# A recurrence of 512 coupled oscillators behind a GRU: VectorE's queue put in another order, the fourth stage's q kept in PSUM, and a clip that waits for ScalarE's square

## The reference

```python
# GRU cell, once per time step, h is [4, 512]
gi = x @ W_ih + b_ih
gh = h @ W_hh + b_hh
r = sigmoid(i_r + h_r);  z = sigmoid(i_z + h_z)
n = tanh(i_n + r * h_n)
h_new = (1.0 - z) * n + z * h

# coupled system, four times per time step, q and p are [4, 512]
i_couple = tanh(q) @ coupling.T
dq = q - q ** 3 / 3.0 - p + drive + i_couple + bias
dp = EPSILON * (q + ALPHA - BETA * p)
# after the four stages
q_next = clip(q + DT / 6 * (dq1 + 2 * dq2 + 2 * dq3 + dq4), -20, 20)
p_next = clip(p + DT / 6 * (dp1 + 2 * dp2 + 2 * dp3 + dp4), -20, 20)
```

## Time and profile before

| | us |
|---|---|
| median of 3 runs | 3659.93 (3659.13 to 3660.63) |
| the profiled execution, its own time | 3661.45 |
| its span, first to last instruction | 3659.7 |
| busy in it: PE | 3546.2 (97%) |
| busy in it: DVE | 2998.4 (82%) |
| busy in it: ACT | 2574.2 (70%) |
| busy in it: POOL | 1507.0 (41%) |

### The profile page before, as it was taken

The page is one execution under the profiler, slowest core; times in us unless marked ns, Lnnn a source line. Parts: engine busy times, 40 slices in busy tenths (PEclk is TensorE's granted clock), DMA queues, the critical chain, the costliest instruction groups (busy, mean ns, idle before and its releaser), DMA issues.

```text
span 3659.7 us, 298613 instructions
## 1 busy us (share of the span) xinstructions
PE 3546.2 (97%) x115469; PEld 3220.4 (88%) x115469; DVE 2998.4 (82%) x20699; ACT 2574.2 (70%) x22689; POOL 1507.0 (41%) x6169
## 2 busy tenths in 40 slices
PE   8989999999999999999999999999999999999978
PEld 4479999999999999999999999999999999999954
DVE  2078888888888888888888888888888888888876
ACT  3257777777777777777777777777777777777753
POOL 0034444444444444444444444444444444444421
PEclk9999999999999999999999999999999999999978
DMA  3000000000000000000000000000000000000001
GB/s 127 23 25 1 1 1 1 1 1 1 1 1 1 1 1 1 1 1 1 1 1 1 1 1 1 1 1 1 1 1 1 1 1 1 1 1 1 1 2 46
DMA packets 9454, 24.45 MB, mean 7 GB/s; under 512 B 557, under 2 KB 601, under 8 KB 8793
## 3 DMA queue, kind: packets, MB, share of 16 engines
q1 hardware_dynamic: 8832, 19.92, 1.5%
q10 hardware_dynamic: 88, 0.02, 0.0%
HBM read 15.75 MB, written 4.19 MB: 5 GB/s over the span
## 4 chain that ended last, share of the span: by engine, by line
PE 79%; DVE 14%; issue 4%; ACT 3%; DVEq 0%; DMA 0%; ACTq 0%; POOL 0%; POOLq 0%
PE psum L1180 43%; PE psum L1138 29%; PE psum L1108 5%; DVE psum L887 2%; DVE tpart L843 2%; DVE gates L776 2%; ACT tpart L571 1%; PE psum L1283 1%; DVE psum L878 1%; DVE psum L866 1%; DVE fresh L795 1%; DVE narg L787 1%; DVE hs L812 1%; ACT tfull L573 1%; DVE hpart L819 0%
## 5 line engine op out<-in xcount | busy, mean ns | idle before, releaser
L1180 PE MATMUL psum<-tpart,cpl 128*128 128x32 f16 x65536 | 1995.8, 177 | 34.1 <-DVE tpart L843 15.0
L1180 PEld LDWEIGHTS psum<-tpart,cpl 128*128 128x128 f16 x65536 | 1788.7, 96 | 150.9 <-DVE tpart L843 41.5
L1138 PE MATMUL psum<-hpart,whh 128*128 128x32 f16 x49152 | 1622.9, 176 | 28.8 <-DVE hpart L819 24.4
L1138 PEld LDWEIGHTS psum<-hpart,whh 128*128 128x128 f16 x49152 | 1404.1, 96 | 91.5 <-DVE hpart L819 30.4
L843 DVE SCALAR_TENSOR_TENSOR tpart<-tfull,tpart 128x8 f16<-128x8 f32 x4096 | 668.4, 163 | 146.6 <-ACT tfull L573 9.9
L571 ACT ACTIVATE tpart<-psum 128x8 f16<-128x8 f32 x3072 | 544.0, 177 | 245.8 <-DVE psum L887 177.2
L887 DVE TENSOR_REDUCE psum<-psum 128x8 f32<-128x24 f32 x3072 | 585.5, 192 | 133.9 <-PE psum L1180 12.2
L573 ACT ACTIVATE tfull<-psum 128x8 f32<-128x8 f32 x3072 | 529.2, 172 | 0.0
L571 ACT ACTIVATE tpart<-qnext 128x8 f16<-128x8 f32 x1024 | 213.9, 209 | 434.6 <-DVE qnext L887 434.5
L535 ACT ACTIVATE qterm<-psum 128x16 f32<-128x16 f32 x3072 | 400.6, 184 | 111.0 <-DVE psum L866 109.1
L374 POOL TENSOR_TENSOR kept<-rz,hs 128x8 f32<-128x8 f32 x1024 | 209.2, 204 | 466.5 <-ACT rz L500 465.6
(11 more groups left out here) (152 smaller groups left out, 4040.5 us busy)
## 6 DMA issues: line engine op xcount, KB each, us to landing
xrow<-in_x_dram SPq DMA_DIRECT2D x4, 1024.0 KB, 11.3
out_dram<-space SPq DMA_DIRECT2D x16, 256.0 KB, 2.0
wih<-in_L_cond_W_ih_dram SPq DMA_DIRECT2D x3, 1024.0 KB, 9.6
space<-in_L_cond_W_hh_dram SPq DMA_DIRECT2D x1, 3072.0 KB, 18.6
space<-in_L_cond_coupling_dram SPq DMA_DIRECT2D x1, 1024.0 KB, 19.2
xrow<-in_cond_dram SPq DMA_DIRECT2D x1, 1024.0 KB, 4.7
wih<-in_L_cond_Wk_dram SPq DMA_DIRECT2D x1, 1024.0 KB, 5.6
wih<-in_L_cond_Wo_dram SPq DMA_DIRECT2D x1, 1024.0 KB, 8.0
```

Of the source, the lines that this page charges most:

```text
L1138: mm = pe.matmul(gate_out[x][:, :, :, c * B:(c + 1) * B], whh[:, w, k, n * P:(n + 1) * P], copies_in(hpart[:, k, :, :]), start=(c == 0 and ...
L1180: mm = pe.matmul(stage_out[a][:, :, :, col:col + B], cpl[:, w, k, n * P:(n + 1) * P], copies_in(tpart[:, s % 2, k, :, :]), start=(col == 0 ...
```

## The change

Five things, all in the loop over time steps:

- The fourth stage's sum goes to `qt` in PSUM like that of the other stages; `qnext` is gone. ScalarE's tanhs and square and VectorE's clip read it there. `lowest`, the clip's lower bound, moves from PSUM to SBUF.
- `clip` stands behind `split_tanh(0, 1)` and `shift_square`, and also waits for ScalarE's square (`sq_ready[0]`).
- `weigh` no longer multiplies by s_h: ScalarE makes `omzs`, omz times s_h, with one new activation of 128x8 for each half (`scaled_omz`), and `weigh` becomes a plain tensor_tensor that waits for it. `split_tanh` also becomes a tensor_tensor.
- In the third stage `base(2)` stands ahead of `sum_gates(1)`. In the fourth, `cubic(3)` stands ahead of `weigh(1)`, `base(3)` ahead of `new_high(1)`, and `h_low(1)` ahead of the first half's sum, where it was behind it. On ScalarE `candidate(1)` stands behind the square of the third stage.
- GpSimd's `keep_part(1)` stands one place later, behind the adding of `sums` in the third stage.

```diff
@@ ScalarE
+            def scaled_omz(x, v):
+
+                act.wait_ge(omz_ready[x], v)
+                act.activation(omzs[:, x, :], omz[:, x, :], ACT.Copy, scale=k_h).then_inc(omzs_ready[x], 1)
...
-                        arg = qt[:, a, :] if s < 3 else qnext[:, a * HC:(a + 1) * HC]
+                        arg = qt[:, a, :]
...
-                        if gru <= T:
-                            candidate(1, gru)
...
+                    if s == 2 and gru <= T:
+                        candidate(1, gru)
@@ VectorE
-                dve.scalar_tensor_tensor(fresh[:, x, :], omz[:, x, :], s_h, cand[:, x, :],
-                                         ALU.mult, ALU.mult).then_inc(fresh_ready[x], 1)
+                dve.tensor_tensor(fresh[:, x, :], omzs[:, x, :], cand[:, x, :], ALU.mult).then_inc(fresh_ready[x], 1)
...
-                dve.tensor_reduce(qt[:, a, :] if s < 3 else qnext[:, a * HC:(a + 1) * HC],
+                dve.tensor_reduce(qt[:, a, :],
...
             def clip(v):
 
                 dve.wait_ge(stage_sum[3][1], v)
+                if v < T:
+                    dve.wait_ge(sq_ready[0], v)
...
+                base(2, now)
+                if gated_step:
                     sum_gates(1, gru)
-                base(2, now)
...
+                cubic(3, now)
                 if gated_step:
                     weigh(1, gru)
-                cubic(3, now)
+                base(3, now)
                 if gated_step:
                     new_high(1, gru)
-                base(3, now)
-                if gated_step:
                     new_h_full(1, gru)
-
-                sum_stage(3, 0, now)
                 if gru < T:
                     h_low(1, gru)
+
+                sum_stage(3, 0, now)
```

More of the change, by code:

```diff
@@ L118, in build @@
         omz = sb("omz", [P, HALVES, HC])
+        omzs = sb("omzs", [P, HALVES, HC])
         gated = sb("gated", [P, HALVES, HC])
@@ L168, in build @@
         scratch_at = bank + 2 * HC
-        cub, square0, lowest = [psum[:, scratch_at + i * KB:scratch_at + (i + 1) * KB] for i in range(3)]
+        cub, square0 = [psum[:, scratch_at + i * KB:scratch_at + (i + 1) * KB] for i in range(2)]
         stage3 = [triple(0, half), triple(bank + half, half)]
@@ L408, in step @@
                         next_uhat(tail)
-                    if s == 1 and gru <= T:
+                    if s == 2 and gru <= T:
                         keep_part(1, gru)
@@ L519, in _ @@
                 sigmoids(1, v)
+                scaled_omz(0, v)
+                scaled_omz(1, v)
                 candidate(0, v)
@@ L591, in step @@
                         stage_terms(0)
+                        if gru <= T:
+                            scaled_omz(0, gru)
                         if 3 <= tail <= T:
@@ L962, in step @@
                     split_tanh(0, 0, tail, tanh_ready[3][0], now)
-                clip(now)
                 if tail <= T:
@@ L966, in step @@
                     shift_square(tail)
+                clip(now)
+                if tail <= T:
                     cubic(0, tail)
```

27 lines of the change are left out of this document (17 added, 10 removed).

## The result

The changed kernel takes 3768.61 us, median of 4 runs (3767.11 to 3769.79), against 3660.23 for the kernel before (4 runs): a ratio of 1.0296, with a 95% interval of 1.0279 to 1.0314. The forecast was 3731 with a range of 3675 to 3780. The sign and the range hold, but the change is +108 us where +71 was forecast. The profiled execution took 3768.42 us with a span of 3766.5, at a mean granted clock of 0.985, where the kernel before has 0.989. The clock is not the cause: from the start of a first stage's products to the end of their 20th matmul it is 0.67 us in either kernel (mean of steps 50 to 450).

What follows compares the result with a forecast made beforehand. The prediction took the ring TensorE, sum, tanhs, split as the bound. Third stage +0.02, fourth up to its sum +0.13, tanhs -0.05, clip +0.04 gave +0.14 us a step, +71 us in all: 3731, range 3675 to 3780.

Steps and rivals of the forecast that it cites:

- the ring: In each time step, the loop TensorE, sum, tanhs, split; claimed to close without slack, TensorE waiting for a split each stage.

Runs made afterwards that it cites:

- experiment 5: The changed kernel in its order, with the clip waiting for ScalarE's square alone except in the last step: 3712.55 us, ratio 1.0131.
- experiment 4: The changed kernel with h_low(1) back between the fourth stage's two sums: 3700.62 us, ratio 1.0113.

## What to carry to other kernels

An instruction laid ahead of a link of the ring costs the wait in front of it, not its own length: put the last instruction of a side chain behind the ring's next link (here 99 us for one place). Where a step makes a new chain, count every wait of every link, and count the chain it must beat from rows of that same stage; waits that another wait already implies should go, and the one that comes last should be the instruction's own. When one of two rings is shortened, compute where the other stands before promising the gain.

## What was not expected of the hardware

- A wait that is an instruction of its own costs VectorE's queue about 0.05 us even when it is long met: the clip starts 0.08 behind its predecessor with none ahead of it (experiment 5), 0.12 with one (the kernel before, 1807.09 to 1807.21) and 0.18 with two (the changed kernel).
- How late an instruction starts behind its releaser depends on whether the wait is its own: it is about 0.04 behind base's end for the first sum (1808.14 to 1808.18), and 0.10 to 0.11 where the wait that comes last is a separate one (clip's end 1807.64 to cub 1807.75). The same cub shows both: in the kernel before, where the shifted square comes last and is its own wait, it starts 0.035 behind that one's end (mean of steps 50 to 450).
- The restart of TensorE's loop is no fixed pause: the next products come 0.74 us behind the start of `h_low(1)`, in eight kernels within 0.01, and as little as 0.55 in the steps without a restart. In the kernel before 0.09 of it shows, in experiment 4 0.19, in the changed kernel nothing. A loop body of four steps brings 254 instruction packets instead of 17, and the kernel is 103 us slower, at a lower granted clock.
- A scalar_tensor_tensor with a scalar from memory is 0.06 longer than a plain tensor_tensor (0.23 against 0.17), and twice a step, in VectorE's chain, this is worth 45 us.
